# Routing in six phases instead of four, row sends spread over thirteen units, in a fused attention and expert kernel

## The reference, cut to what matters

```
probs = softmax(xt @ router_w)
top1 = argmax(probs);  top2 = argmax(logits without top1)
loc1 = cumsum(m1) - 1.0
loc2 = cumsum(m2) - 1.0 + m1.sum()
m1 = m1 * (loc1 < C);  m2 = m2 * (loc2 < C)
slot1 = (loc1 * m1).sum(-1);  slot2 = (loc2 * m2).sum(-1)
xin = einsum('tec,td->ecd', dispatch, xt)
```

## Time and profile before

| | us |
|---|---|
| median of 3 runs | 1950.85 (1948.93 to 1954.16) |
| the profiled execution's own time | 1948.95 |
| its span, first to last instruction | 1947.2 |
| mean granted TensorE clock | 0.879 of full speed |
| TensorE matmuls busy | 1548.6 (80%) |
| VectorE busy | 1297.8 (67%) |
| GpSimd busy | 1078.7 (55%) |
| ScalarE busy | 966.4 (50%) |

### The profile page before, as it was taken

The page is one execution under the profiler, slowest core; times in us unless marked ns, Lnnn a source line. Parts: engine busy times, 40 slices in busy tenths (PEclk is TensorE's granted clock), DMA queues, the critical chain, the costliest instruction groups (busy, mean ns, idle before and its releaser), DMA issues. The chain is left out here.

```text
span 1947.2 us, 46256 instructions
## 1 busy us (share of the span) xinstructions
PE 1548.6 (80%) x17646; PEld 941.7 (48%) x17646; DVE 1297.8 (67%) x3322; ACT 966.4 (50%) x2039; POOL 1078.7 (55%) x1712
## 2 busy tenths in 40 slices
PE   5648788876599999854798599999999999744993
PEld 4532333345255555433576355555555555423772
DVE  7348888782688878734421688888888887544324
ACT  4215667732166677520233166777777776411331
POOL 3447766505378775545355376555757765552552
PEclk9977999977599999865799599999999999755996
DMA  8443322204333223100343442332323322001445
GB/s 288 112 131 104 90 82 80 75 23 123 114 120 104 82 88 99 42 28 23 114 138 98 138 126 84 92 100 78 113 84 98 97 81 83 26 23 56 141 130 156
DMA packets 233185, 188.08 MB, mean 97 GB/s; under 512 B 30044, under 2 KB 221368, under 8 KB 232326
## 3 DMA queue, kind: packets, MB, share of 16 engines
q1 hardware_dynamic: 222582, 166.36, 28.5%
q0 software_dynamic: 10240, 18.76, 2.9%
q10 hardware_dynamic: 144, 0.00, 0.0%
HBM read 104.34 MB, written 80.74 MB: 95 GB/s over the span
## 5 line engine op out<-in xcount | busy, mean ns | idle before, releaser
L1008 DVE TENSOR_REDUCE mx<-PS 128x2 f32<-128x512 f32 (+3 forms) x1408 | 784.2, 612 | 189.0 <-PE PS L648 137.5
L858 ACT ACTIVATE pt<-PS 128x512 f32<-128x512 f32 (+2 forms) x1408 | 667.6, 537 | 312.1 <-PE PS L648 227.6
L665 PE MATMUL PS<-ka,qa 52*128 52x256 bf16 (+3 forms) x2048 | 461.7, 305 | 65.2 <-DVE mx L1008 47.4
L781 PE MATMUL PS<-qa,ka 55*128 55x512 bf16 (+3 forms) x1792 | 459.7, 321 | 41.3 <-DMA qa<-nm 17.8
L725 PE MATMUL PS<-pt,vs 128*32 128x512 f32 (+3 forms) x3584 | 349.6, 481 | 2.3 <-issue 1.5
L648 PE MATMUL PS<-mask_q,identh 64*128 64x64 bf16 x3072 | 299.5, 193 | 1.5 <-issue 1.4
L648 PE MATMUL PS<-mask_k,identh 64*128 64x64 bf16 x3072 | 299.0, 192 | 0.9 <-issue 0.9
L781 PEld LDWEIGHTS PS<-qa,ka 55*128 55x128 bf16 x1792 | 166.9, 94 | 273.7 <-issue 119.3
L648 PEld LDWEIGHTS PS<-mask_k,identh 64*128 64x128 bf16 x3072 | 249.2, 97 | 51.7 <-issue 6.8
L648 PEld LDWEIGHTS PS<-mask_q,identh 64*128 64x128 bf16 x3072 | 252.4, 98 | 31.0 <-issue 8.9
L1161 POOL CAST nm<-nm 16x128 bf16<-16x128 f32 x128 | 36.2, 283 | 340.1 <-ACT nm L890 329.3
(11 more groups left out here) (249 smaller groups left out, 2333.4 us busy)
## 6 DMA issues: line engine op xcount, KB each, us to landing
pt<-in_f_w SPq DMA_DIRECT2D x96, 256.0 KB
qa<-q_parts SPq DMA_DIRECT2D x256, 96.0 KB, 2.3
ka<-k_parts SPq DMA_DIRECT2D x192, 96.0 KB, 2.3
q_parts<-parts SPq DMA_DIRECT2D x32, 384.0 KB, 3.4
k_parts<-parts SPq DMA_DIRECT2D x24, 384.0 KB, 2.6
xn<-y_rows SPq DMA_DIRECT2D x32, 256.0 KB, 3.2
hid<-y_rows SPq DMA_DIRECT2D x32, 256.0 KB, 3.7
q_parts<-parts SPq DMA_DIRECT2D x32, 256.0 KB, 3.2
```

What stands on the lines that cost most here:

```text
L665: mm = pe.matmul(PS[:, bank, i * n:(i + 1) * n], k.qa[rows, b % 2, g, h // 2, qb * P:(qb + 1) * P], k.ka[rows, b % 2, g, h // 2, 0:n], sta ...
L781: mm = pe.matmul(PS[:, bank, i * n:(i + 1) * n], k.ka[rows, b % 2, g, h // 2, kb * P:(kb + 1) * P], k.qa[rows, b % 2, g, h // 2, q0:S], st ...
L858: nc.scalar.activation(k.pt[:, u % 2, at[c]:at[c] + len(heads) * n], PS[:, SC_BANK + c % RING, 0:len(heads) * n], ACT.Exp, scale=SCORE_SCA ...
L1008: nc.vector.tensor_reduce(out, PS[:, MX_BANK + t % RING, 0:len(heads) * n] .rearrange("p (h n) -> p h n", n=n), AX.X, ALU.max).then_inc(s. ...
```

## The change

Both passes with `route1` route in six phases instead of four: (0, 8), (8, 16), then four tiles at a time up to 32. The marks have phases of their own, three of them (`SENT_MARKS`). The chosen events of the routing are now a table of phase, unit and slot (`SENT_CHOICES`); phase 0 is chosen in U-16 to U-14, phase 1 in U-8 to U-6, phase 2 in U-4 and U-3, phase 3 in U-2, phase 4 in U-1, phase 5 in the tail. Fronts are transposed two batches behind instead of three (`FRONT_LAG`), which moves front 4 from U-4 and U-3 to U-5, and each earlier front one batch forward. Sends start in U-13 with one tile (two DMAs) in each unit. In the tail, PE does `ranks` before the first `occupants`, and DVE's rows of marks stand after the last front. In the marks, phase 0 has 16 tiles.

```diff
-SENT_PHASES = ((0, 8), (8, 16), (16, 28), (28, 32))
+SENT_PHASES = ((0, 8), (8, 16), (16, 20), (20, 24), (24, 28), (28, 32))
+SENT_MARKS = ((0, 16), (16, 28), (28, 32))
...
-    SENT_IN = {-6: (0, 1), -5: (1, 4), -4: (4, 5), -3: (5, 8), -2: (8, 12), -1: (12, 16)}
+    SENT_IN = {t - 13: (0, t, t + 1) for t in range(8)}
+    SENT_IN |= {-5: (1, 8, 11), -4: (1, 11, 14), -3: (1, 14, 16), -2: (2, 16, 20), -1: (3, 20, 24)}
+    SENT_CHOICES = (("choose", (0, 0), -16, 8), ("choose", (0, 1), -15, 8), ("choose", (0, 2), -14, 4),
...
+                    ("choose", (2, 0), -4, 8), ("choose", (2, 1), -3, 3), ("choose", (2, 2), -3, 6),
+                    ("ranks", 2, -3, 8), ("find", 2, -3, 9),
+                    ("choose", (3, None), -2, 5), ("ranks", 3, -2, 11), ("find", 3, -2, 11),
+                    ("choose", (4, None), -1, 1), ("ranks", 4, -1, 8), ("find", 4, -1, 9), ("mark", 0, -1, 10))
+    FRONT_LAG = 2 if r.sent else 3
...
             tail("o_T", U // 2 - 1)
             for name in ("ctx_T", "out"):
                 tail(name, NB - 1)
-            occupants(pe, k, r, 0)
+            if not r.sent:
+                occupants(pe, k, r, 0)
             for name in ("f_T", "f_l"):
                 tail(name, NB - 1)
             if r.sent:
-                occupants(pe, k, r, 1)
+                ranks(pe, k, r, LAST)
+                occupants(pe, k, r, 0)
             else:
                 ranks(pe, k, r, LAST - 1)
-            ranks(pe, k, r, LAST)
-            for j in (LAST - 1, LAST):
+                ranks(pe, k, r, LAST)
+            for j in (1, 2):
                 occupants(pe, k, r, j)
...
             tail("o_T", U // 2 - 1)
             if r.sent:
                 mark_tiles(nc, k, route, r, 1)
-            mark_rows(nc, k, route, r, 0)
+            else:
+                mark_rows(nc, k, route, r, 0)
             tail("out", NB - 1)
             front(NB - 1)
             if r.sent:
-                mark_rows(nc, k, route, r, 1)
+                mark_rows(nc, k, route, r, 0)
                 dve.wait_ge(*s.gl_free.at(r.phases[LAST][1] // TB))
                 choose(nc, k, route, r, LAST)
                 find_ranks(nc, k, route, r, LAST)
-                for j in (LAST - 1, LAST):
-                    mark_tiles(nc, k, route, r, j)
-                    mark_rows(nc, k, route, r, j)
+                mark_rows(nc, k, route, r, 1)
+                mark_tiles(nc, k, route, r, 2)
+                mark_rows(nc, k, route, r, 2)
```

More of the change, by code:

```diff
@@ L540, in attention @@
                 "q": 11, "v": 11, "out": 5, "value1": 11, "moments": 4, "f_moments": 4, "f_T": 8, "f_l": 11,
-                "late0": 0, "late2": 6, "late_root": 0, "choose": 6, "ranks": 5, "mark": 6, "f_rows": 0,
-                "choose0": 8, "ranks0": 8, "find0": 9, "choose1": 7, "choose2": 9, "choose3": 1, "ranks1": 9,
-                "find1": 10, "choose4": 1}
+                "late0": 0, "late2": 6, "late_root": 0, "f_rows": 0}
         last_front = (11, 8, 11, 3, 8, 11)
@@ L550, in attention @@
                 "q": 7, "v": 7, "out": 7, "moments": 3, "f_moments": 3, "f_T": 5, "f_l": 7,
-                "late0": 0, "late2": 4, "late_root": 0, "choose": 5, "ranks": 4, "mark": 5, "f_rows": 0}
+                "late0": 0, "late2": 4, "late_root": 0, "choose": 5, "ranks": 4, "find": 5, "mark": 5, "f_rows": 0}
         last_front = (7, 5, 7, 3, 6, 7)
@@ L593, in order @@
             first = (0, 1, 3)[g]
-            fronts = [(name, FIRST + i, slot) for (name, i), slot in zip(names[g], last_front[first:])]
+            fronts = [(name, FIRST + i, slot) for (name, i), slot in zip(names[g], last_front[first:])
+                      if i > NB - 2 - FIRST - FRONT_LAG]
         if g == 0 and b:
@@ L606, in order @@
         if r.sent:
[L607 to L616, removed]
+            fronts += [(name, n, slot) for name, n, unit, slot in SENT_CHOICES if u == U + unit]
         else:
             if u == U - 2:
-                events += [("choose", 0)]
+                events += [("choose", (0, None))]
             if u == U - 1:
-                events += [("ranks", 0), ("mark", 0)]
+                events += [("ranks", 0), ("find", 0), ("mark", 0)]
         plan = []
@@ L827, in _ @@
                         tail(name, n)
-                    elif name in ("ranks0", "ranks1"):
+                    elif name == "ranks" and r.rank_banks[n] == MISC:
                         take_misc()
@@ L1079, in _ @@
                         front(n)
[L1080 to L1088, removed]
+                    elif name == "choose":
+                        j, step = n
+                        if not step:
+                            dve.wait_ge(*s.gl_free.at(r.phases[j][1] // TB))
+                        choose(nc, k, route, r, j, (0, 1, 2) if step is None else (step,))
+                    elif name == "find":
                         find_ranks(nc, k, route, r, n)
-                    elif name in ("choose", "choose4"):
-                        dve.wait_ge(*s.gl_free.at(r.phases[n][1] // TB))
-                        choose(nc, k, route, r, n)
                     elif name == "mark":
-                        find_ranks(nc, k, route, r, n)
                         dve.wait_ge(*s.pv_done.at(U - 1))
-                        mark_tiles(nc, k, route, r, 0)
+                        mark_tiles(nc, k, route, r, n)
             tail("o_T", U // 2 - 1)
@@ L1246, in _ @@
                 if r.sent and u - U in SENT_IN:
-                    send(pool, k, r, int(u >= U - 2), range(*SENT_IN[u - U]))
+                    phase, first, end = SENT_IN[u - U]
+                    send(pool, k, r, phase, range(first, end))
             if r.sent:
```

28 lines of the change are left out of this document (17 added, 11 removed).

## The result

The changed kernel takes **1925.11 us** (median of 4 runs, 1924.52 to 1933.9) against 1950.67 for the kernel before: a ratio of 0.9873, with a 95% interval from 0.9845 to 0.9902. On another chip, beside the experiments, the ratio was 0.9888 (0.9873 to 0.9904). The prediction said 1931, in a range from 1898 to 1955, and faster with a chance of 0.70.

The account below looks back on a forecast made before the run. The prediction took the pass's end as a serial chain, with POOL's long rows of sends delaying PE's signals to ACT and DVE. Terms -13 + 0 - 8 + 11 = -10 a pass, -20 for two, gave 1931 us, range 1898 to 1955.

Parts of the forecast that it names:

- Tail: From R to the last `slot`: 8 sends instead of 24 there; -13 us a pass, bounds -16 and -5.
- R: Reference time: the `slot` of the phase found in U-1, at 1725.81 in the kernel before's third pass.
- the transposes come at R + 21.2: Tail step: the last front's transposes, before at R + 18.7, move +2.5 us for the larger mark of phase 0.
- After the last `slot`: From the last `slot` on: PE has 128 matmuls of `occupants` instead of 64; gain at most 2 us, taken as 0.
- less than that: After the last `slot`: POOL's eight sends need 10.2 + 0.8 us, less than PE's 14.1 us for 128 matmuls.
- U-2 and U-1: T to R, 36.2 us before: two rows of 8 sends, shorter choice; -8 us a pass, bounds 0 and -14.
- U-13 to U-3: Units where sends rise from 16 to 32: sum 11.5 + 3 - 3 + 0, +11 us a pass, from +2 to +21.
- Larger gain: Rival 1, chance 0.20: rows of eight end before the hold, pairs cost nothing; -26 us a pass, 1899 us.
- The hold stays in U-2 and U-1: Rival 2, chance 0.15: PE waits for choices of phases 3 and 4; T to R 0, -2 a pass, 1947 us.
- T: Reference time: the last `max_split` of the pass, at 1689.65 in the kernel before's third pass.
- Slower: Rival 3, chance 0.15: spread sends cost more in the units than the tail gives; 1977 or about 1968 us.
- The change does not do what it says: Rival 4, chance 0.07: the copy's 15.3 us wait is not the sends'; tail gives 0, about 1951 us.

Follow-up runs that it names:

- m14_change_again: The changed kernel as it is, measured again on the same chip as m13_pause_again: 1930.29 us, ratio 0.9888.
- m4_drop: The changed kernel without the 16 sends of phase 0, their rows not delivered: 1915.45 us, ratio 0.9816.
- m3_rows8: The changed kernel with phase 0's 16 sends in two rows of eight (U-12 and U-9) instead of eight pairs: 1957.51 us, ratio 1.0025.
- m7_behind: The kernel before, its 24 sends put behind the last front's logits and nothing in their place: 1966.28 us, ratio 1.0079.
- m5_pause: The kernel before, with one wait added: inside a phase, after every eight sends, POOL waits until they have landed: 1919.15 us, ratio 0.9825.
- m1_row24: The changed kernel with tiles 16 to 28 one phase again, its 24 sends in one row behind U-1: 1927.77 us, ratio 0.9863.
- m13_pause_again: m5_pause run once more, on the same chip as m14_change_again: 1910.68 us, ratio 0.9802.

## Why the prediction was right, point by point

The direction, the main mechanism and the time (1925 for 1931) held. The balance of one pass, forecast against the two passes measured:

1. **Tail**: forecast -13, from R + 44.6 to R + 31.8; measured R + 26.9 and R + 28.0, -17.7 and -16.6, just past the bound of -16. The step that failed is "the transposes come at R + 21.2". They came at R + 16.3 and R + 17.4. In the third pass the mark of 16 tiles took 5.4 us (forecast 6) and the reciprocal came at R + 7.1, 2 us later than before (forecast 2.5). But the 18.7 us taken as clean held late signals of their own: from the reciprocal to the transposes it was 13.7 us before, and 10.3 now. Before, DVE took up the matmuls of `out` 2.4 us behind their end, 1.5 of it idle, and the transposes started 1.4 us behind the last `xn`; both waits are gone. The sum also left out that 1.3 us of `mark_rows` moved behind the front. From the copy to the last slot it took 9.4 us, as forecast.
2. **After the last slot**: forecast 0; measured the same, 15.8 us to the end of the index for 15.4. But the working named the wrong bound. PE's 128 matmuls took 15.5 us beside the sends (forecast 14.1) and end 0.1 us before the index, yet the next part does not wait for them: its first load comes 6.6 to 7.5 us behind the start of POOL's last send in every kernel here, also in the six passes with pauses in which the index begins 0.3 to 8.0 us before that send. The forecast took the eight sends as "less than that", which is true of their issue and leaves out the time to that load. So the 0 came out for another reason than the one given: the same eight sends follow the last `slot` in both kernels.
3. **U-2 and U-1**: forecast -8; measured -8.6 and -9.9, and -8.6 and -6.0 in m14_change_again. Finding phase 3 still waited 7.81 us for PE.
4. **U-13 to U-3**: forecast +11; measured +10.8 and +12.8, and +14.7 and +16.3 in m14_change_again. The size is right within this scatter, its make-up is open. The 0.72 us a send came from a unit with a group of six; pairs cost 0.4 to 0.7 by the two measurements, 6 to 11 us for the 16 in place of 11.5. The term that was too small is, by elimination, the moved fronts and choices, put at 0 to 2 because DVE has idle time in the units: m4_drop, without these sends, pays 4.6 and 5.3 us. The idle time is there, but PE waits 2.1 us for DVE's maxima where the scan stands ahead of them.

The rivals. *Larger gain* had the end of the pass nearly right (-26.3 and -26.5 for its -30), but pairs are not free. *The hold stays in U-2 and U-1* fell by T to R. *Slower* fell for pairs and has the right direction for rows: m3_rows8 pays 1.3 to 1.4 us a send, more than its 1.1, and ends at 1957, not at 1977, since T to R still shrank. *The change does not do what it says* fell by m7_behind.

Three small slips in the working changed nothing: the end of the eight sends' hold is R + 14.0 by its terms, not R + 14.2; the bound of -14 for U-2 and U-1 is not what two rows of 10.2 us and 3 us give, 36.2 less 23.4, or -12.8; and half of rival 2 with rival 4 is 0.145, not 0.13.

What the prediction missed lies beside its terms. It took the spreading as the means by which the gain comes. m5_pause shows that the gain is had in place, by breaking the rows behind T; the change pays 11 to 16 us a pass in the units for it. m1_row24 shows that beside the spread the split phase gives nothing, though its row of 24 still held PE in one pass of two.

## What to carry to other kernels

Before work is moved away from a stall, try breaking up the cause where it stands: a wait for the DMAs already issued, after every eight indirect sends, cost 2 us each and gained 31 to 40 us. Sends in pairs beside a full PE cost 0.4 to 0.7 us each and in rows of eight 1.3 to 1.4, so price a send by the size of its group. And before a wait is read as "bound by the engine named", compare several kernels: here the stretch behind POOL's last send was constant within 2 us, whatever the profile named as releaser.

## What the runs showed of the hardware

Beside a long row of indirect DMAs from POOL, PE itself nearly stops at times. In the second pass of the kernel before, PE goes at full pace until 895.6, and then issues one matmul for each send or fewer (PE, then POOL):

```profile
894.07 1.50 PE L474 MATMUL PS<-work,pt 128*128 128x64 bf16 x11
896.14 0.27 PE L474 MATMUL PS<-work,pt 128*128 128x64 bf16 x1 [0.57 <-issue]
897.54 0.27 PE L474 MATMUL PS<-work,pt 128*128 128x64 bf16 x1 [1.13 <-issue]
898.98 0.27 PE L474 MATMUL PS<-work,pt 128*128 128x64 bf16 x1 [1.16 <-issue]
...
908.86 0.90 PE L195 MATMUL PS<-ident,xn 128*128 128x128 f32 x3 [6.79 <-remote]
```

```profile
895.14 0.97 POOL L415 DMA_INDIRECT xe_rows<-xn,slot  x1 [0.30 <-issue]
...
908.47 0.97 POOL L415 DMA_INDIRECT xe_rows<-xn,slot  x1 [0.30 <-issue]
```

So "late signals" was half the picture: matmuls already issued signal late, and later ones are not issued. It began about 14 sends into this row, where PE had little to do, and about 6 us into the row of m3_rows8, where PE was full; with rows of eight (m5_pause, m13_pause_again) the last front's copy waits 0.04 to 1.9 us, with rows of twelve the last slot comes 8 to 11 us later than in m5_pause. A pause of 2 us until the issued sends have landed ends it. DVE and ACT keep their pace beside the sends (0.42 us for a mark of 128x512, 0.78 us for the copy `xfT`) and only miss PE's signals. The transfers do not pile up: in the DMA records of the kernel before, the last packet of each send starts 1.8 to 2.4 us after the send, for the 24th as for the first. What fills up or is held in the way of PE's signals and of its issue stays open. A run with half the bytes in each send gave no result, so bytes and number of descriptors were not separated. The row of 24 does not hit the same step each time: the same stretch took 37.0 and 29.4 us in two passes of one run.
